# A layer's set-up rearranged: small products to GpSimd, transfers and an exponential moved forward

## The reference

```python
xn = layernorm(x)
# attention, 16 heads of 16 columns, windows of 64 steps back
disp, val = xn @ W_disp, xn @ W_val
strain = window(disp) - disp                     # for each of the 64 offsets
bond   = gelu(strain @ W_strain + rel @ W_pos) @ W_bond
damage = sigmoid(gelu(strain @ W_dmg + b_dmg) @ W_dmg_out + b_dmg_out)
att    = softmax(mask(bond - 10 * damage)) @ window(val)
# experts, 16, of which 4 per token
t = xn * rsqrt(mean(xn * xn) + eps) * scale
route = softmax over the 4 best of (t @ gate_w.T + gate_b)
moe   = sum over chosen experts e of route[e] * (swiglu(t @ w1[e] + b1[e]) @ w2[e] + b2[e])
x = x + att @ W_cproj + moe
```

## Time and profile before

| what | value |
|---|---|
| median of 3 runs | 1132.99 us (1130.6 to 1134.23) |
| profiled execution | 1132.02 us |
| its span on the core | 1130.3 us |
| TensorE, VectorE, ScalarE, GpSimd busy | 86%, 80%, 70%, 47% |
| mean granted TensorE clock | 0.95 of full speed |

### The profile page before, as it was taken

The page is one execution under the profiler, slowest core; times in us unless marked ns, Lnnn a source line. Parts: engine busy times, 40 slices in busy tenths (PEclk is TensorE's granted clock), DMA queues, the critical chain, the costliest instruction groups (busy, mean ns, idle before and its releaser), DMA issues. The chain is left out here.

```text
span 1130.3 us, 23604 instructions
## 1 busy us (share of the span) xinstructions
PE 972.2 (86%) x9302; PEld 518.5 (46%) x9302; DVE 908.1 (80%) x1006; ACT 788.0 (70%) x859; POOL 532.7 (47%) x549
## 2 busy tenths in 40 slices
PE   6687777889788899999998579998999999989897
PEld 4422222333466344433343578534646465555533
DVE  7987888899776999999997777677686667476856
ACT  3689999999764799999998642431366656555573
POOL 6088888528506558888887204407710000000172
PEclk9899999999988899999999789997799999999999
DMA  9891000012187222222211684000314335432121
GB/s 312 226 367 36 31 34 33 24 40 67 46 266 216 75 61 70 74 75 75 75 53 38 187 296 139 1 0 26 97 57 122 99 116 140 122 103 85 38 59 45
DMA packets 102212, 113.75 MB, mean 101 GB/s; under 512 B 11509, under 2 KB 86737, under 8 KB 98385
## 3 DMA queue, kind: packets, MB, share of 16 engines
q1 hardware_dynamic: 93876, 98.15, 28.6%
q0 software_dynamic: 6656, 13.91, 3.6%
q10 hardware_dynamic: 1571, 0.20, 0.1%
HBM read 66.48 MB, written 42.59 MB: 96 GB/s over the span
## 5 line engine op out<-in xcount | busy, mean ns | idle before, releaser
L260 DVE SCALAR_TENSOR_TENSOR ring<-AD,PT 128x1808 f32<-128x1808 f32 (+15 forms) x128 | 282.2, 2221 | 28.6 <-PE LG L983 26.8
L983 PE MATMUL LG<-ring,lred 128*32 128x456 f32 (+15 forms) x2048 | 235.3, 579 | 0.0
L266 POOL DMA_INDIRECT ys<-rows,goali x80 | 160.5, 2006 | 81.8 <-DVE rows L867 49.4
L2336 DVE TENSOR_REDUCE MX<-SS 128x2 f32<-128x1024 f32 x119 | 144.5, 1218 | 55.6 <-PE SS L2053 55.5
L2266 ACT ACTIVATE EX<-SS 128x1024 f32<-128x1024 f32 x128 | 130.3, 1031 | 77.6 <-PE SS L2053 77.1
L923 ACT ACTIVATE ring<-ring 128x3680 f32<-128x3680 f32 (+15 forms) x47 | 161.1, 3429 | 3.6 <-DVE ring L260 3.6
L1008 PE MATMUL SD<-DSf,eyes 99*32 99x456 bf16 (+15 forms) x1280 | 97.1, 380 | 69.4 <-ACT ring L928 64.7
L929 ACT ACTIVATE ring<-ring 128x1824 f32<-128x1824 f32 (+15 forms) x80 | 145.7, 1822 | 0.0
L776 POOL DMA_INDIRECT xs<-rows,sloti x64 | 123.9, 1935 | 29.6 <-issue 19.2
L1970 POOL DMA_INDIRECT XN<-ys,sloti x16 | 16.3, 1017 | 246.7 <-PE SS L2063 242.2
L260 DVE SCALAR_TENSOR_TENSOR ring<-AD,bdmg 128x1808 f32<-128x1808 f32 (+15 forms) x48 | 106.4, 2216 | 0.0
(11 more groups left out here) (430 smaller groups left out, 1689.5 us busy)
## 6 DMA issues: line engine op xcount, KB each, us to landing
ring<-band SPq DMA_DIRECT2D x6, 2048.0 KB, 12.2
w1s<-in_L_ffn_W SPq DMA_DIRECT2D x39, 256.0 KB, 2.9
w2s<-in_L_ffn_W SPq DMA_DIRECT2D x39, 256.0 KB, 2.9
band<-Z SPq DMA_DIRECT2D x8, 1024.0 KB
xl<-xs SPq DMA_DIRECT2D x20, 272.0 KB, 2.9
xs<-Z SPq DMA_DIRECT2D x5, 1024.0 KB, 9.9
w1s<-w1d SPq DMA_DIRECT2D x80, 64.0 KB
w2s<-w2d SPq DMA_DIRECT2D x80, 64.0 KB
```

Source lines behind the costliest of these rows:

```text
L260: return v.scalar_tensor_tensor(out=tile[:, s, :, t0:T], in0=AD[:, s, :, j + t0:j + T], scalar=extra, in1=AD[:, s, :, PAD + t0:PAD + T], o ...
L266: pool.indirect_dma_start(ys0[:, :], bass.IndirectOffsetOnAxis(ap=goali[:, 4 * n + a:4 * n + a + 1], axis=0), yo[:, n % 2, a, :], None, bo ...
L983: mm = pe.matmul(LG[32 * b:32 * b + 32, par, s, t0:T], lred[:, s, n % 4, :], ring[:, slot, s, b, t0:T], start=(n % 4 == 0), stop=(n % 4 == 3))
L2336: v.tensor_reduce(MX[:, t, p // 2, hh:hh + 2], pairs_of(b, name), AX.X, ALU.max).then_inc(freed[slot], 1)
```

## The change

It makes four moves. The memset and the eight products for `lred` leave VectorE and go to GpSimd, behind its `iota`s and ahead of its wait for the scaled rows, with a wait for the small weights. The transfers of parts 1 and 2 go from SyncE's list in the first main block to the end of its list in the set-up block. On ScalarE the exponential goes ahead of weight groups 4 and 5, and the second cast ahead of groups 5, 6 and 7. In the main loop, the tile counts go behind the second strain of item 0, which stood behind them.

```diff
@@ set-up block, SyncE
             sp.wait_ge(mlp_sb, 8)
             sp.dma_start(w2d.rearrange("e p c -> p e c"), w2T[:]).then_inc(d_small, 16)
+            send_parts(sp, 0, parts0, (1, 2))
@@ set-up block, GpSimd
             pool.iota(index[:], pattern=[[0, 32]], base=0, channel_multiplier=1, allow_small_or_imprecise_dtypes=True)
+            link(pool.memset(lred[:], 0.0))
+            pool.wait_ge(d_attn_w, 16 * 10)
+            for s in range(2):
+                for a in range(4):
+                    pool.tensor_tensor(lred[:, s, a, a:32:4], mask8[:], wcol[:, s:s + 1].to_broadcast([P, HG]), ALU.mult)
             pool.wait_ge(tf_ready, B)
@@ set-up block, VectorE
             v.tensor_copy(PT[:], S[0][:, 256:256 + WIN]).then_inc(small_dve, 1)
-            link(v.memset(lred[:], 0.0))
-            for s in range(2):
-                for a in range(4):
-                    last = v.tensor_scalar(lred[:, s, a, a:32:4], mask8[:], wcol[:, s:s + 1], None, ALU.mult)
@@ set-up block, ScalarE
             turned_weights(2)
             turned_weights(3)
-            turned_weights(4)
-            turned_weights(5)
             act.wait_ge(exp_ready, 1)
             act.activation(route[:], route[:], ACT.Exp).then_inc(exp_done, 1)
+            turned_weights(4)
+            act.wait_ge(parts_dve, 1)
+            act.copy(parts0[1], rest0).then_inc(parts_act, 1)
+            turned_weights(5)
             turned_weights(6)
             turned_weights(7)
-            act.wait_ge(parts_dve, 1)
-            act.copy(parts0[1], rest0).then_inc(parts_act, 1)
@@ main loop, SyncE, g == 0
-                    send_parts(sp, 0, parts0, (1, 2))
@@ main loop, VectorE, g == 0
                     strain(0, 0, 0)
+                    strain(0, 0, 1).then_inc(strain_ready, 1)
                     expert_tiles()
-                    strain(0, 0, 1).then_inc(strain_ready, 1)
```

## The result

The changed kernel took 1138.99 us (median of 8 runs, 1134.06 to 1146.98), the kernel before 1131.39 us beside it (8 runs, 1121.96 to 1134.23). The ratio is 1.0085, 95% interval 1.0054 to 1.0116; in a second comparison of 12 runs it was 1.0070 (1.0042 to 1.0098). So it is slower, by 7.6 and 7.7 us between the medians. I had forecast 2.7 us and "slower" with a chance of 0.32 only: the sign of the sum was right, its size was not, and the measured time lies above the stated range (1131.5 to 1138.5).

What follows compares the result with a forecast made beforehand. ScalarE was taken to bound the first loop, so a set-up delay carries over: block start +3.6 us, less 0.96 us of TensorE's wait, gives +2.7 us on 1132.99, so 1135.7 us; range 1131.5 to 1138.5.

Steps and rivals of the forecast that it cites:

- 1. Logits' weights: Set-up block: moving memset and eight products off VectorE lets its sum into ACC start 1.5 us earlier.
- d: How much earlier than 27.65 us VectorE's sum into ACC starts; taken as 1.5 us, ends 0.2 and 4.6.
- both holds: Two VectorE products stopped until GpSimd's mask copy and AD memset end, 1.3 and 1.4 us over pure work.
- Rival A: Set-up block: GpSimd's eight products each hold VectorE through the shared port; d 0.2, sum +4.0 us (1137.0); chance 0.20.
- 2. ScalarE's order: Set-up block: exponential and second cast go first, so weight group 7 is done at 41.18 us against 38.19.
- 3. The eight transfers: End of set-up block: SyncE issues them behind w2d, ends last at 46.95 us; next block +3.6 us late.
- eight issues 5.11: SyncE's set-up list: issuing the eight transfers takes 5.11 us, 0.64 each, as measured in the next block before.
- rival D: Set-up block's end: SyncE is not last, issues faster than 0.64 us or not waited for; about 1133.0; chance 0.07.
- What it was to buy: First main block: TensorE's wait for the last part goes, so ScalarE's product comes 0.96 us sooner.
- rival C: First main block: parts land no earlier for TensorE, w2d being ahead; the 0.96 us wait stays; +3.6 us, 1136.6; chance 0.06.
- Rival B: Loop's first strains: TensorE's clock stays at 2.4 GHz, gaining 2.7 us; sum 0.0, 1133.0; chance 0.13.
- 4. Tile counts: First main block: first gelu starts some 0.8 us sooner, only ScalarE's wait for TensorE grows; nothing either way.

Runs made afterwards that it cites:

- e10: Changed kernel with SyncE's w2d write moved behind the eight transfers of the parts; ratio 1.0027 to the kernel before, block start 30.79 us.
- e5: Kernel before with only the tile counts moved behind the second strain of item 0; ratio 1.0005 to the kernel before.
- e2: Kernel before with only the eight transfers moved into the set-up block; ratio 1.0034 to the kernel before.
- e3: Kernel before with only the logits' weights moved to GpSimd; ratio 0.9991 to the kernel before, block start 24.84 us.

## Why the prediction was right or wrong

**1. Logits' weights: right.** d was put at 1.5, and the changed profile has 10.44 - 8.95 = 1.49 us. That it fits so closely is luck: the working gave 1.2 for the case in which both holds stay. Both holds are there again, with other work in them:
```profile
21.19 1.97 POOL L386 COPY mt<-mt 64x2048 f32<-64x2048 f32 x1 [0.68 <-DVE rows L420]
21.31 1.88 DVE L453 TENSOR_SCALAR eyes<-ident 32x32 bf16<-32x32 f32 x1
...
24.80 1.16 DVE L457 CAST bpart<-brow 3x128 bf16<-3x128 f32 x1
25.34 0.54 POOL L394 MEMSET AD<- 128x504 f32 x1
```
A product of `eyes` ends at 23.19, 0.03 after the mask copy, and a cast of `bpart` at 25.96, 0.08 after the memset. They are 1.88 and 1.16 us long, against 1.54 and 1.61 before. That they belong to GpSimd's instructions, as argued, is read from these ends. Rival A is wrong in that the eight products did not add holds that cost anything. Its d of 0.2 does not come out of its own condition either: with both holds staying, 1.2 less eight times 0.2 is -0.4.

**2. ScalarE's order: right in kind, a little short.** The chain was forecast to end group 7 at 41.18, 23.97 us behind the small weights; it ended at 43.06, 24.53 behind them. The 0.56 us are mostly the last fill, taken as 0.70 us from TensorE at its high clock (1.00 from 33.0 to 34.1). TensorE had stood for 3.04 us, the granted clock was 0.50, and the four transposes alone took 1.12:
```profile
41.31 1.12 PE L560 MATMUL su<-ident,w2r 128*128 128x128 f32 x4 [3.04 <-ACT w2T L502]
42.46 0.60 ACT L502 ACTIVATE w2T<-su 128x512 f32<-128x512 f32 x1 [0.72 <-PE su L560]
```

**3. The eight transfers: the step that failed.** That SyncE would end last and hold all engines was right, and so was the place. The term "eight issues 5.11" in SyncE's sum was mis-sized: it measured 7.59 us (43.57 to 51.16), because w2d ahead of them was still under way (e10). I took 0.64 us an issue from a stretch in which nothing large was on the queue, and put the issues behind w2d; rival D even asked whether they would be faster. The opposite was to be read in the kernel before. Here is SyncE in its first 13 us, with the two 1 MB reads of the experts' weights under way:
```profile
2.95 0.51 SPq L323 DMA_DIRECT2D w1r<-in_L_ffn_mlp_w  x1
3.67 3.65 SPq L324 DMA_DIRECT2D w2r<-in_L_ffn_mlp_w  x1
7.36 4.97 SPq L325 DMA_DIRECT2D wval<-in_L_attn_W_val  x1
```
The first issue took 0.51 us; a second large one behind it took 3.65 and the small one behind both 4.97. The drain and the meeting took 0.69 us from the last issue's end instead of 0.43. So the block start was forecast 3.6 us late and came 6.97 late. Of the difference 2.48 us are the issues', 0.56 group 7's and 0.26 the drain's, together 3.30. e10 took the first of these away alone and got 2.5 us back.

What it was to buy, 0.96 us, came to 0.51: ScalarE's product starts 9.40 us into the block instead of 9.91. The parts were there (rival C is wrong), but the counting took 5.58 us instead of 5.07: TensorE had stood for 6.42 us ahead of it, and the granted clock was at 0.50, the 1.2 GHz level, until about 56.8, 4.9 us into the block. In the kernel before it had stood for 1.21 us, and the clock rose at about 47.4, 3.9 us into the block. The first two rows are the kernel before, the others the changed one:
```profile
45.52 5.07 PE L1025 MATMUL PH<-chosen_key,attT 128*128 128x240 f32 x30
...
46.70:48.70 2.00, 2.00 (x12) 1.96 (x11) 2.00 (x2) 0.25 (x1) 0.00 (x0) 0.82 1.02 182
```
```profile
53.00:55.00 2.00, 2.00 (x6) 1.66 (x7) 2.00 (x2) 0.10 (x1) 0.19 (x4) 0.50 1.14 241
55.00:57.00 2.00, 2.00 (x8) 1.95 (x7) 1.93 (x6) 0.99 (x1) 0.00 (x0) 0.56 0.99 414
```
By the loop's end even that half is not seen: 256.0 us against 255.6, where all twelve profiles lie between 254.9 and 257.0. Whether those 0.5 us are lost again in the loop or are only below the scatter stays open. Rival B's gain did not come. The first strains behind the counting ran at the high level (0.57 us a group at 60.19), but from 64 to 66 us the granted clock was 0.50 again, 16 logits' matmuls took 3.23 us (2.88 in the earlier trace rows) and the strains ahead of them, for which TensorE had waited 0.47 us for ScalarE, 0.94 us a group:
```profile
64.64 0.94 PE L1009 MATMUL SD<-DSf,eyes 99*32 99x452 bf16 x8 [0.47 <-ACT ring L932]
...
66.13 3.23 PE L984 MATMUL LG<-ring,lred 128*32 128x452 f32 x16
```

**4. Tile counts: right**, nothing (e5). The first gelu starts 4.16 us into the block instead of 4.89, 0.73 sooner where some 0.8 was forecast, and ScalarE's wait for TensorE's product grows from 1.80 to 2.03 us.

**The range and the chances.** The range's end, 1138.5, lay just under the measured median; it had been set by rivals that did not come true, not by the price of an issue. The price of an issue was the one cost taken with no bounds, because eight of eight rows agreed; all eight were from one stretch.

## What to carry to other kernels

Issuing a transfer is work of its queue with a price of its own, and at a meeting of all engines an otherwise idle queue is as good as any to be last: count its issues to the drain, in order. Take the price of an issue from a stretch with the same load on the queue; directly behind a large transfer that is still under way it was up to 2.8 times as long (1.66 and 0.60 us), though not for each issue (e2). Moving work forward pays when the engine that ends the block gets shorter (e3, -1.5 us), not when a waiting one is filled up to the end.

## What the runs showed that was not expected

- The issue of a 128 KB transfer takes 0.60 us with nothing large ahead of it, 1.66, 1.37, 1.10 and 0.76 in a row directly behind a 1 MB write, and 0.89 to 0.96 on the mean when two queues issue at once (3.85 us for four on ScalarE).
- A cast of 3 rows of 128 elements took 1.16 us when it ended with GpSimd's memsets, and 0.22 to 0.36 otherwise.
- The landing of small weights at the start differs by 2.1 us, and a stage that reads 2 MB pieces from DRAM by 5.2 us, between profiles of nearly the same program. Two profiles' spans do not tell 3 us from 7; one interval inside the trace, counted from an event that all kernels share, repeats within 0.04 us.
